# One-hot columns by four comparisons with a row number per partition, in place of one with two broadcast operands

## The reference

```
e = jnp.stack([tbl_0[ids[:, 0]], tbl_1[ids[:, 1]], ..., tbl_25[ids[:, 25]]], axis=1)
combined = jnp.concatenate([dense[:, None, :], e], axis=1)        # 2048 x 27 x 128
interactions = jnp.einsum('bfd,bgd->bfg', combined, combined)
z = jnp.concatenate([dense, interactions[:, iu, ju]], axis=1)     # iu, ju: upper triangle, 351 pairs
h = jnp.concatenate([z, dense], axis=1)                           # 607 wide
h = jnp.maximum(h @ W_top1 + b_top1, 0.0)                         # 512
h = jnp.maximum(h @ W_top2 + b_top2, 0.0)                         # 256
y = h @ W_top3                                                    # 1
```

## Time and profile before

| | |
|---|---|
| median of three runs | 485.12 us (484.35 to 487.92) |
| the profiled execution | 483.39 us |
| its span, first to last instruction | 481.6 us |
| mean granted PE clock | 0.957 |
| busy: PE, DVE, ACT, POOL | 416.1, 292.1, 241.0, 292.1 us |

### The profile page before, as it was taken

One profiled execution on the slowest core, in us unless ns is written; L12 is line 12 of the kernel. 1 busy time (PEld: TensorE's weight loads), 2 busy tenths in 40 slices (PEclk: granted clock), 3 DMA queues, 4 the chain that ended last, 5 costly groups with the idle time before them and its releaser, 6 DMA issues.

```text
span 481.6 us, 8713 instructions
## 1 busy us (share of the span) xinstructions
PE 416.1 (86%) x3384; PEld 392.4 (81%) x3384; DVE 292.1 (61%) x446; ACT 241.0 (50%) x558; POOL 292.1 (61%) x263
## 2 busy tenths in 40 slices
PE   1776978789899997989996989989996998988997
PEld 1765968679897897979985889979996898977976
DVE  4996856584577555774755836774674745733441
ACT  2534555284347444474434734474451834547562
POOL 0786565547687565666776666876686766772000
PEclk9999998899999997999997999997997999997999
DMA  7996152215222242214232153221322122110000
GB/s 196 249 258 176 46 108 65 65 29 97 73 61 62 61 95 56 72 27 87 76 76 49 31 93 76 66 62 46 89 76 57 42 73 77 40 50 17 1 1 0
DMA packets 24608, 35.92 MB, mean 75 GB/s; under 512 B 6296, under 2 KB 18720, under 8 KB 24568
## 3 DMA queue, kind: packets, MB, share of 16 engines
q1 hardware_dynamic: 16376, 18.57, 17.1%
q0 software_dynamic: 8192, 16.79, 13.7%
HBM read 35.33 MB, written 0.01 MB: 73 GB/s over the span
## 4 chain that ended last, share of the span: by engine, by line
PE 55%; DVE 14%; ACT 11%; issue 10%; another core or an unknown queue 8%; DMA 1%; SPq 0%; DVEq 0%; ACTq 0%
PE gram_ps L420 14%; PE x_ps L401 12%; PE x_ps L402 10%; DVE hot L882 9%; PE x_ps L384 5%; ACT x L640 5%; PE tail_ps L461 3%; PE tail_ps L462 3%; PE tail_ps L463 3%; ACT pairs L640 3%; DVE gram L860 2%; ACT gram L640 2%; PE tail_ps L453 2%; DMA x<-in_tbl_dram 1%
## 5 line engine op out<-in xcount | busy, mean ns | idle before, releaser
L350 POOL DMA_INDIRECT rows<-in_tbl_dram,ids_sb x256 | 291.3, 1138 | 147.5 <-issue 57.4
L401 PE MATMUL x_ps<-hot,table_hi 125*128 125x256 f32 x640 | 170.0, 301 | 41.0 <-DVE hot L882 19.4
L882 DVE TENSOR_TENSOR hot<-ids_all,row_f 125x1024 fp32r<-125x1024 int32 x120 | 142.6, 1221 | 49.4 <-PE x_ps L402 22.4
L401 PEld LDWEIGHTS x_ps<-hot,table_hi 125*128 125x128 f32 x640 | 127.1, 199 | 48.4 <-issue 32.6
L402 PE MATMUL x_ps<-hot,table_lo 125*128 125x256 f32 x640 | 163.4, 290 | 0.0
L402 PEld LDWEIGHTS x_ps<-hot,table_lo 125*128 125x128 f32 x640 | 127.5, 199 | 0.0
L420 PE MATMUL gram_ps<-x 128*108 128x108 f32 x1024 | 115.5, 267 | 6.4 <-issue 5.4
L420 PEld LDWEIGHTS gram_ps<-x 128*108 128x108 f32 x1024 | 108.9, 182 | 8.7 <-issue 6.5
L640 ACT ACTIVATE picked<-x_ps 128x256 f32<-128x256 f32 x80 | 30.6, 382 | 100.1 <-PE x_ps L402 46.5
L860 DVE COPY gram<-gram_ps 44x208 f32<-44x208 f32 (+1 forms) x120 | 44.3, 370 | 38.1 <-remote 21.2
L640 ACT ACTIVATE gram<-gram_ps 44x208 f32<-44x208 f32 (+3 forms) x136 | 45.8, 337 | 30.7 <-PE gram_ps L420 15.7
(11 more groups left out here) (76 smaller groups left out, 352.3 us busy)
## 6 DMA issues: line engine op xcount, KB each, us to landing
ids_all<-in_selected_ids_dram SPq DMA_DIRECT2D x80, 128.0 KB
rows<-in_tbl_dram,ids_sb POOLq DMA_INDIRECT x256
x<-in_tbl_dram SPq DMA_DIRECT2D x6, 448.0 KB
stage<-in_tbl_dram SPq DMA_DIRECT2D x3, 448.0 KB
rows<-in_r_dense_features_dram SPq DMA_DIRECT2D x16, 64.0 KB
stage<-in_W_pairs_dram SPq DMA_DIRECT2D x1, 702.0 KB
stage<-in_W_dense_dram SPq DMA_DIRECT2D x2, 256.0 KB
stage<-in_W_dram SPq DMA_DIRECT2D x1, 512.0 KB
```

The source lines that it names most:

```text
L350: pool.indirect_dma_start(out=rows[t][:, slot, :], out_offset=None, in_=tables[GATHERED[slot - 1]], in_offset=bass.IndirectOffsetOnAxis(ap ...
L401: first = pe.matmul(bank, table_hi[j][:, c, :], v, start=(c == 0), stop=False)
L882: dve.tensor_tensor(hot[h][:], ids_all[0:VK, j % IDS, :].unsqueeze(1).broadcast_to([VK, HALF, MACRO]), row[0:VK, these].unsqueeze(2).broad ...
```

## The change

`row_start` and the extra counts for its bank are gone. For all macro tiles the comparison reads `row_f` in SBUF. What was one DVE instruction for a half (`tensor_tensor`, 125 x 1024 elements, both operands broadcast) is now four `tensor_scalar` instructions of 125 x 256, each with one column of `row_f` as its scalar for each partition. Only the last of the four raises `hot_ready`.

```diff
@@ tail_at
             i = LAST_BANKS[q]
-            return i, LAST_BANKS[:q].count(i) + (m * (T_USES // 2) + 1 if i < 2 else 0)
-        return q % 2, m * (T_USES // 2) + (q // 2 + 1)
+            return i, LAST_BANKS[:q].count(i) + (m * (T_USES // 2) if i < 2 else 0)
+        return q % 2, m * (T_USES // 2) + q // 2
@@ psum
-        row_start = tail_ps[1][:, 0:VC]
@@ scalar
-            act.nop().then_inc(tail_moved[0], 1)
@@ build_hot
-                    these = slice(h * HALF, (h + 1) * HALF)
-                    row = row_start if m < 2 else row_f
-                    dve.tensor_tensor(
-                        hot[h][:], ids_all[0:VK, j % IDS, :].unsqueeze(1).broadcast_to([VK, HALF, MACRO]),
-                        row[0:VK, these].unsqueeze(2).broadcast_to([VK, HALF, MACRO]),
-                        ALU.is_equal).then_inc(hot_ready, 1)
+                    for c in range(HALF):
+                        row = row_f[0:VK, h * HALF + c:h * HALF + c + 1]
+                        last = dve.tensor_scalar(hot[h][:, c, :], ids_all[0:VK, j % IDS, :], row, None, ALU.is_equal)
+                    last.then_inc(hot_ready, 1)
@@ vector, the start
             copy(row_f[:], row_i[:]).then_inc(rows_ready, 1)
-            copy(row_start, row_i[:]).then_inc(rows_ready, 1)
-            dve.wait_ge(rows_ready, 2)
+            dve.wait_ge(rows_ready, 1)
@@ vector, after macro tile 0
-            dve.wait_ge(hot_ready, 2 * (2 * NS))
-            dve.nop().then_inc(tail_moved[1], 1)
```

## The result

| | median (range, runs) | span profiled | granted PE clock |
|---|---|---|---|
| before, beside it | 486.52 us (484.35 to 491.25, 4) | 481.6 us | 0.957 |
| after | 501.31 us (499.16 to 506.22, 4) | 497.4 us | 0.966 |

The ratio is 1.0305, with an interval of 1.0192 to 1.0417: slower, where 480 us was forecast and the range ended at 490.

What follows compares the result with a forecast made beforehand. PE was taken as the bound, with DVE full in the start. Terms -4.0 + 1.5 - 2.4 - 1.0 + 0.4 = -5.5 us from 485.12 gave 479.6, forecast as 480 us (chance 0.48), range 475.5 to 490.

Steps and rivals of the forecast that it cites:

- the one on the gathers: In the start, DVE's back-to-back instructions would keep POOL's gathers out, making some 8 of 21 late: +1.5 us, between 0 and 4.
- the earlier start: In the start, DVE needs 2.81 us per table in place of 3.40, so PE starts at 37.2 instead of 41.17: -4.0 us.
- a half "begun late": In the steady part, PE's largest hole, 3.82 us, was put down to DVE beginning a half late at 255.79, not its length.
- The piece: Each DVE comparison of 256 elements starts 0.21 us after the last, so a half takes 0.84 us instead of 1.13.
- The rival with the scalar: Each DVE piece pays 0.07 to 0.09 us for its pointer, a half stays 1.12 to 1.20: 485 us, chance 0.17.
- Two elements at a time: DVE's int32 comparison with one tensor source in SBUF runs at the rate of the casts, two elements at a time.
- POOL between the pieces: Rival: gathers get between DVE's pieces, each delaying the next by 0.94 us; +7.3 in the start, +2 later: 494 us, chance 0.08.
- The steady part: Behind the start, PE's waits of about 0.8 us go (-2.4), others shrink (-1.0), +0.4 given back.
- The Trainium skill's rule: In SBUF, a two-port DVE operation and a GpSimd operation exclude one another for a whole instruction; weighed as speaking against the change.

Runs made afterwards that it cites:

- e6: The changed kernel with the old comparison of 1024 columns, its row numbers read from SBUF for all macro tiles: 432.95 us, ratio 1.0119 to the kernel before.
- g4: The changed kernel comparing with constants 0 to 7, first row number subtracted from the ids once per table, right rows picked: 488.79 us, ratio 0.9979 to before.
- e7: The changed kernel with constants in place of the row-number pointers, so other rows are picked: 421.56 us, ratio 0.9849 to the kernel before.
- e11: The kernel before with table_lo alone cut into four subtractions of 256 columns, on a faster chip: 430.02 us, ratio 1.0038 to before.
- e1: The changed kernel with the first 20 gathers of macro tile 0 spaced, two for each table: 480.68 us, ratio 1.0111 to the kernel before.
- g1: The changed kernel unaltered, run a third time, on a slower chip: 502.06 us, ratio 1.0337 to the kernel before.
- g2: The changed kernel with all gathers released by DVE's hot_ready counts, two per table in the start, on a slower chip: 528.29 us, ratio 1.0874 to before.
- e2: The kernel before with table_lo alone cut into four subtractions of 256 columns: 491.6 us, the kernel before 478.32 us on that chip.
- e4: The changed kernel with two comparisons of 512 columns per half instead of four of 256, other rows picked: 487.4 us, ratio 1.026 to before.
- e9: The changed kernel unaltered, run again on a faster chip: 429.46 us, ratio 1.0041 to the kernel before.
- g3: The kernel before, unaltered, run beside the changed kernel on a slower chip: 485.21 us, ratio 1.0012.
- e3: The old comparison for m < 2, the new four comparisons from m = 2 on: 481.35 us, the kernel before 478.32 us on that chip.
- e5: The changed kernel with spaced gathers in the start and a POOL memset of 128 x 702 per pair of gathers: 439.46 us, ratio 1.0267 to before.
- e12: The changed kernel with all gathers paced by DVE's hot_ready instead of PE's count, on a faster chip: 427.82 us, ratio 0.9986 to before.
- h1: The changed kernel comparing with constants 0 to 7 after one subtraction per table, right rows picked, on a faster chip: 423.3 us, ratio 0.9889 to before.
- h2: As h1, with the first twenty gathers of m = 0 let go two by two: 424.57 us, ratio 0.9898 to the kernel before.

## Why the prediction was wrong

- **The step that failed** is the one on the gathers: "Two DVE instructions back to back let nothing in the earlier trace rows. After the change nearly all of DVE's work in the start keeps POOL out." In the sum it and the earlier start stood as -4.0 and +1.5 us; the start came out at +16.9. The gathers became faster, 0.95 us each, every 1.25. The row it rested on the earlier trace rows has two-operand instructions of 1.2 us that overlap by their ends. Pieces with a pointer overlap too (345 ns long, 0.26 us apart), and yet POOL gets in among them. The sentence holds for the long ones (e6: 1.97 us a gather), at times for constants 0.21 apart (g4: 2.7 to 3.1, but e7 mostly 0.94 to 1.24) and for short two-operand pieces in e11 (2.05). What decides between them is open.
- **What it led to** was in none of the cases: gathers without pause, and PE's counts told late: 16.9 us in the start, more than the 15.8 between the spans. That the train brings the stall is shown by e1 (spaced: gone), g1 against g2 (the same on one chip: 58.99 and 42.44) and g2 behind its start (train elsewhere: stall elsewhere); e2 adds that the new comparison is not needed for it. The sign was in the earlier trace rows: the 5.62 us of DVE's wait named "remote" ahead of 255.79 is such a late count, and I took it for a half "begun late" without asking what it waited for.
- **The piece** was mis-sized: 0.26 us from start to start, (2.19 - 0.345) / 7, not 0.21. The rival with the scalar was half right: the pointer costs 0.06 of it (e7, g4), so a half is 1.05, between 0.84 and 1.13. Two elements at a time held (e4).
- **POOL between the pieces** was priced at 0.7 us and more a gather, from its full 0.94. It is 0.17. With three gathers a table that is 3.75 us against the 2.81 forecast and 3.40 before. So -4.0 us in the start is +2 without any late count, and the whole change 1.6 us slower (e9). This rival had the mechanism, the sign and the place, but put 7.3 us on the start where 2 were measured, and had with 0.08 the least of the chances. That its 494 us came nearer to the 501 than the forecast did is luck: late counts made those.
- **The steady part**, -3.0 forecast, gave 1.1 us less in the first pair of traces. On chips with late counts this is not to be told from their scatter (g1 lost 6.3 there against g3); e3 shows no gain either, as far as its few executions tell.
- **The Trainium skill's rule** ("SBUF — State Buffer", Who interferes with whom), weighed in the prediction, has a DVE operation in a two-port mode and a GpSimd operation shut one another out for a whole instruction. That fits g4 in part; in the changed kernel a gather takes 0.95 us among the pieces, hardly more than its 0.94 alone, and delays them by 0.17. The same section has an instruction with two inputs in SBUF contend with a GpSimd instruction that reads SBUF; e6 agrees, with 1.97 us a gather.

Open: what makes a count late. The ends of matmuls are modelled, so part of a late count could be a late end. It can't be all: PE starts the second half of selection 4 at 35.18, behind the first in its own order, and DVE is told of the first at 43.11, 7.9 us later. Nor is it known what differs between the chips at 428 us and those at 478 to 486, where the kernel before shows late counts too. The prediction was made from a trace of the second kind. Whether it is the missing pauses or the number of gathers in a stretch that matters is open as well. A limit on gathers under way was not tried, since it needs a wait that races.

## What to carry to other kernels

Before an instruction is cut into pieces, look at what its length kept away: here one long instruction spaced another engine's DMAs, and nothing in the change spoke of them. A wait that no record explains is a finding, not noise: follow it before the argument rests on the row behind it. And a change of 1% is to be judged on more than one chip, since it was 1.03 twice and 1.004 on another.

## What was not expected of the hardware

- In trains of 8 to 21 indirect DMAs that follow every 1.25 us, counts of PE are told 4 to 13 us late in the first trace of the changed kernel and up to 16.5 us late in g1, and two counts whose matmuls ended 7.4 us apart are told in one moment (43.1 in the first trace). Every trace from a chip where the kernel before takes 478 to 486 us has waits of DVE and ACT named "remote", e1 behind its start, and no trace of e5 to e12, h1 and h2 has one. DVE's counts reach PE within 0.15 us in the rows above.
- The same kernel before takes 427.9 us on one chip and 485.7 on another. PE is busy for 415.1 us in g3, the kernel before on the slower one, and for 391.8 in e9, the changed kernel on the faster, with a granted clock of 0.975 and 1.000.
- `tensor_scalar` with a pointer for each partition starts every 0.26 us at 256 elements, with a constant every 0.21, (1.71 - 0.27) / 7.
- A gather holds DVE's short pieces up by 0.17 us, a memset on POOL of 0.70 us (128 x 702) by 1.0 (e5 against e1).
